# A fused two-layer transformer block on one core: the row maxima of the attention made 22 tiles ahead, from products of 32 rows on pairs of TensorE's row groups

## What is computed

```python
x = x + attention(layernorm(x))      # 16 heads of 8, rotary positions, softmax over 1024 keys
x = x + fp4_ffn(layernorm(x))        # blockwise quantised linear layers, silu(gate) * up
x = x + state_space(layernorm(x))    # softplus, a scan over the sequence, 32 states
x = x + moe(layernorm(x))            # 8 experts, the two best of each token
# the attention, for each batch b and head h:
attn = softmax(einsum('bhqd,bhkd->bhqk', q, k) * scale)
out  = einsum('bhqk,bhkd->bhqd', attn, v)
```

## Time and profile before

| what | us |
|---|---|
| median of 3 runs (1035.95 to 1038.92) | 1038.09 |
| the profiled execution | 1043.72 |
| its span of instructions | 1041.9 |
| ahead of the first product for maxima | 0 to 51.6 |
| maxima of pass 0 | 51.6 to 89.4 |
| passes 0 to 7 | 89.4 to 474.3 |
| FFN, state space and experts | 474.3 to 1041.9 |

### The profile page before, as it was taken

The page is one execution under the profiler, slowest core; times in us unless marked ns, Lnnn a source line. Parts: engine busy times, 40 slices in busy tenths (PEclk is TensorE's granted clock), DMA queues, the critical chain, the costliest instruction groups (busy, mean ns, idle before and its releaser), DMA issues. The chain is left out here.

```text
span 1041.9 us, 12586 instructions
## 1 busy us (share of the span) xinstructions
PE 858.3 (82%) x3695; PEld 401.7 (39%) x3703; DVE 848.1 (81%) x779; ACT 589.2 (57%) x913; POOL 273.1 (26%) x147
## 2 busy tenths in 40 slices
PE   5589999989999949985575565877777479999998
PEld 2212222222222212222444422322223266888886
DVE  6699888878888838855868789999999873888886
ACT  2304777767777727784132453444444166888885
POOL 3700000000000000010100157899999710122110
PEclk9857999999999969998586578899999877999999
DMA  7450010110102030002100232455455002232111
GB/s 177 126 138 1 11 57 12 57 47 31 44 28 57 12 102 12 11 11 62 34 0 6 81 106 83 159 178 170 167 172 178 2 0 84 62 110 71 60 61 41
DMA packets 37976, 73.51 MB, mean 71 GB/s; under 512 B 7298, under 2 KB 21626, under 8 KB 36890
## 3 DMA queue, kind: packets, MB, share of 16 engines
q1 hardware_dynamic: 37922, 72.82, 22.7%
HBM read 62.50 MB, written 8.85 MB: 68 GB/s over the span
## 5 line engine op out<-in xcount | busy, mean ns | idle before, releaser
L1004 DVE TENSOR_REDUCE nmax<-ps 128x1 f32<-128x1024 f32 x256 | 301.2, 1219 | 59.5 <-PE ps L1333 59.5
L765 ACT ACTIVATE prob<-ps 128x512 f32<-128x512 f32 x512 | 265.7, 605 | 139.4 <-PE ps L1352 139.2
L1333 PE MATMUL ps<-ks,qs 96*128 96x512 bf16 x512 | 206.6, 417 | 30.5 <-DVE nmax L1004 18.1
L1352 PE MATMUL ps<-qs,ks 96*128 96x512 bf16 x512 | 195.3, 390 | 7.2 <-ACT prob L765 3.3
L683 POOL TENSOR_TENSOR hc<-hst,cbr 128x1024 f32<-128x1024 f32 x64 | 152.6, 2408 | 10.1 <-DVE hst L1127 7.4
L1127 DVE TENSOR_TENSOR_SCAN hst<-ps,dbx 128x1024 f32<-128x1024 f32 x64 | 144.8, 2279 | 0.2
L1531 PE MATMUL ps<-hc,ident 128*128 128x512 f32 x256 | 128.9, 628 | 8.4 <-POOL hc L683 7.4
L1369 PE MATMUL ps<-prob,vq 128*16 128x512 f32 x1024 | 134.1, 601 | 0.8 <-ACT prob L765 0.7
L868 ACT ACTIVATE ps<-dt,a_neg 128x1024 f32<-128x1024 f32 x64 | 71.5, 1117 | 99.7 <-DVE hst L1127 99.6
L1216 DVE TENSOR_TENSOR act_l<-act_t,act_h 128x1024 fp32r<-128x1024 f32 x64 | 91.0, 1431 | 36.6 <-ACT act_h L937 36.6
L1352 PEld LDWEIGHTS ps<-qs,ks 96*128 96x128 bf16 x512 | 49.7, 99 | 165.6 <-ACT prob L765 117.7
(11 more groups left out here) (178 smaller groups left out, 1043.6 us busy)
## 6 DMA issues: line engine op xcount, KB each, us to landing
cbr<-s_dram SPq DMA_DIRECT2D x64, 512.0 KB, 4.1
gate<-c_dram SPq DMA_DIRECT2D x8, 1024.0 KB, 7.4
qs<-q_dram SPq DMA_DIRECT2D x18, 288.0 KB
ks<-k_dram SPq DMA_DIRECT2D x54, 96.0 KB
o_dram<-o_sb SPq DMA_DIRECT2D x16, 256.0 KB, 2.0
wf<-in_L_ffn_w SPq DMA_DIRECT2D x8, 256.0 KB, 2.9
wfq<-in_L_ffn_w SPq DMA_DIRECT2D x8, 256.0 KB, 3.1
q_dram<-parts SPq DMA_DIRECT2D x16, 96.0 KB, 1.9
```

The source lines that it names most:

```text
L765: nc.scalar.activation(prob[:, n % 8], ps[:, 4 + (first + n) % 3], ACT.Exp, scale=ATT_SCALE).then_inc(s_exp, 1)
L1004: nc.vector.tensor_reduce(nmax[:, half, n:n + 1], ps[:, 2 * (t % 2):2 * (t % 2) + 2, :], AX.XY, ALU.max, negate=True).then_inc(s_max, 1)
L1333: mm = nc.tensor.matmul(ps[:, 2 * (t % 2) + kk], qs[p][:, half, h, q * P:(q + 1) * P], ks[p][:, kk, h, :], start=True, stop=True)
L1352: nc.tensor.matmul(ps[:, 4 + (first + n) % 3], ks[p][:, kt // 4, j, kt % 4 * P:(kt % 4 + 1) * P], qs[p][:, half, j, :], start=True, stop=T ...
```

## The change

1. The maxima run 22 tiles ahead (LEAD), not 32. Ahead of pass 0 stand 22 tiles; steps 0 to 4 of each pass make tiles 22 to 31 of the pass itself, and steps 5 to 15 make tiles 0 to 21 of the next pass. So pass 7 has ten tiles in its first five steps.
2. From pass 1 on, a tile is made differently (`score_pair`): two heads by 512 keys, each head one product with 32 rows (two bfloat16 parts of q against two of k, all four combinations), in two of the four groups of 32 rows of TensorE, into two banks. There are as many tiles as before, with two products each. VectorE reduces a tile to two columns (one for each head), and a new operation on 128x16 takes the minimum over the two key halves (the values are negated). Pass 0 keeps the old form.
3. The operands `qm` and `km` lie head by head in groups of 32 rows and are filled by `load_heads`: 24 DMAs for a pass (12 for each half), each of 16 or 32 rows of 1 KB.
4. SyncE's queue is put in a new order: in pass it first the maxima of its own second half, then the 24 small loads for pass it+2, the output half, the maxima of the next pass's first half, the second output half, then `load` for it+3. The second four of the stores of q and k parts go into pass 0. The last three passes load nothing.
5. The reload of batch 0's sums is split: `load_out(0)` stands in pass 4, `load_denominators(0)` in pass 5, and VectorE inverts the denominators between the maxima of passes 5 and 6.
6. TensorE and SyncE have all passes written out, without a loop. ScalarE keeps its loop of two rounds, VectorE loops over passes 1 to 5.
7. In pass 7 `project_out(0)` goes from step 1 to 6, `turn_weights` from 8 to 12, and `turn_first_x` behind the pass; ScalarE's counterparts move likewise.

```diff
+PASS_TILES = QUAD * KT
+LEAD = 22
+        HEAD_LOADS = 16 * 2 * 3 * QUAD
+            def load_heads(it, p, f):
+                for h in range(QUAD):
+                    q, k = (t[bass.ds(it, 1), f].rearrange("o n (d h) t -> (o n d) h t", h=QUAD)[0:2 * HD, h]
+                            for t in (q_dram, k_dram))
+                    sp.dma_start(km[p][32 * h:32 * h + 32, f], k.unsqueeze(0).to_broadcast([2, 2 * HD, BANK])).then_inc(s_qm[p], 16)
+                    for a in range(2):
+                        sp.dma_start(qm[p][32 * h + 16 * a:32 * h + 16 * a + 16, f],
+                                     q[HD * a:HD * a + HD].unsqueeze(0).to_broadcast([2, HD, BANK])).then_inc(s_qm[p], 16)
...
-            for p in range(SETS):
-                load(p, p)
-            for u in range(CHUNKS, 2 * CHUNKS):
-                store_parts(u)
-            for n in range(CHUNKS):
-                sp.wait_ge(s_parts_out[n], 16 * QUAD * 2)
+            load(0, 0)
+            load(1, 1)
+            load_heads(1, 1, 0)
             store_maxima(0, 0, 0)
-            store_maxima(0, 0, 1)
-            def one_pass(it, p, more, again=None):
+            load_heads(1, 1, 1)
+            load(2, 2)
+            def one_pass(it, p, more, again=None, meanwhile=None):
+                store_maxima(it, p, 1)
+                if it + 2 < PASSES:
+                    for f in range(2):
+                        load_heads(it + 2, (p + 2) % SETS, f)
+                if it == 0:
+                    for u in range(CHUNKS, 2 * CHUNKS):
+                        store_parts(u)
+                    for n in range(CHUNKS):
+                        sp.wait_ge(s_parts_out[n], 16 * QUAD * 2)
+                store_out(it, 0)
                 if more:
                     store_maxima(it + 1, (p + 1) % SETS, 0)
-                store_out(it, 0)
+                if meanwhile:
+                    meanwhile()
+                store_out(it, 1)
                 if again is not None:
                     sp.wait_ge(s_pv, STEPS * (it + 1))
                     load(again, p)
-                store_out(it, 1)
-                if more:
-                    store_maxima(it + 1, (p + 1) % SETS, 1)
...
+            for it in range(PASSES):
+                one_pass(it, it % SETS, it < PASSES - 1, it + SETS if it + SETS < PASSES else None,
+                         {4: lambda: load_out(0), 5: lambda: load_denominators(0)}.get(it))
...
                         if whole:
                             nc.vector.tensor_reduce(nmax[:, half, n:n + 1], ps[:, 2 * pair:2 * pair + 2, :],
                                                     AX.XY, ALU.max, negate=True).then_inc(s_max, 1)
+                        else:
+                            nc.vector.tensor_reduce(nmax_k[:, half, kk, 2 * pair:2 * pair + 2, qt], ps[:, 2 * pair:2 * pair + 2, :],
+                                                    AX.X, ALU.max, negate=True).then_inc(s_max, 1)
...
+                        nc.vector.tensor_tensor(nmax[:, half], nmax_k[:, half, 0].rearrange("p h q -> p (h q)"),
+                                                nmax_k[:, half, 1].rearrange("p h q -> p (h q)"), ALU.min).then_inc(s_mstep, 1)
...
             inverse_denominators(0)
+            maxima(PASSES - 2)
             maxima(PASSES - 1)
...
+            def score_pair(it, p, u):
+                half, qt, kk, pair = u // 16, u % 16 // 4, u % 4 // 2, u % 2
+                pe.wait_ge(s_max, 32 * it + u - 1)
+                for n in range(2):
+                    rows = slice(32 * (2 * pair + n), 32 * (2 * pair + n + 1))
+                    mm = nc.tensor.matmul(ps[:, 2 * pair + n], qm[p][rows, half, qt * P:(qt + 1) * P],
+                                          km[p][rows, kk, :], start=True, stop=True)
+                mm.then_inc(s_score, 1)
...
-                        for t, kk in todo[len(todo) * j // 4:len(todo) * (j + 1) // 4]:
-                            score_half(it + 1, (p + 1) % SETS, t, kk)
+                        for tile in todo[len(todo) * j // 4:len(todo) * (j + 1) // 4]:
+                            if tile[0] == 0:
+                                score_half(*tile, 0)
+                                score_half(*tile, 1)
+                            else:
+                                score_pair(*tile)
...
-            for t in range(32):
+            for t in range(LEAD):
                 score_half(0, 0, t, 0)
                 score_half(0, 0, t, 1)
-            with pe.Fori(0, PASSES // SETS) as r:
-                for p in range(SETS):
-                    one_pass(SETS * r + p, p, 4 * STEPS * p, True, r + 1 + (p + 1) // SETS)
-            one_pass(PASSES - 2, 0, 0, True, PASSES // SETS + 1)
+            for it in range(PASSES - 1):
+                one_pass(it, it % SETS, 4 * STEPS * it, True, it // SETS + 1)
...
-            one_pass(PASSES - 1, 1, 4 * STEPS, False, between={1: lambda: project_out(0), 8: turn_weights, 12: turn_first_x})
+            one_pass(PASSES - 1, 1, 4 * STEPS, False, PASSES // SETS + 1, between={6: lambda: project_out(0), 12: turn_weights})
+            turn_first_x()
```

More of the change, by code:

```diff
@@ L127, in build_kernel @@
         qs, ks = ([pair[n] for pair in stacks] for n in range(2))
+        qm, km = ([sb(f"{w}{n}", [P, 2, BANK], BF16) for n in range(SETS)] for w in ("qm", "km"))
         prob = sb("prob", [P, 8, BANK])
@@ L136, in build_kernel @@
         nmax = sb("nmax", [P, 2, 16])
+        nmax_k = sb("nmax_k", [P, 2, 2, QUAD, 4])
         nmax_p = sb("nmax_p", [P, 32], BF16)
@@ L140, in build_kernel @@
         den = sb("den", [P, BATCH, HEADS * SEQ // P])
[L141 removed]
+        rden = sq[:].rearrange("p (b t) c -> p b (t c)", b=BATCH)
         num = sb("num", [P, TOKENS])
@@ L229, in build_kernel @@
         s_qk = [sem(f"s_qk{n}") for n in range(SETS)]
+        s_qm = [sem(f"s_qm{n}") for n in range(SETS)]
         s_score = sem("s_score")
@@ L564, in load_out, with load_denominators @@
                 sp.dma_start(num[:, b * SEQ:(b + 1) * SEQ], rows[:, 0:HD]).then_inc(s_num, 16)
+            def load_denominators(b):
                 sp.wait_ge(s_rden, b + 1)
@@ L570, in load_out @@
                 sp.sem_inc(s_ready, 1)
-            with sp.Fori(0, PASSES // SETS) as r:
-                for p in range(SETS):
-                    one_pass(SETS * r + p, p, True, (SETS * r + p + SETS) % PASSES)
-            load_out(0)
-            one_pass(PASSES - 2, 0, True)
-            one_pass(PASSES - 1, 1, False)
+            for it in range(PASSES):
+                one_pass(it, it % SETS, it < PASSES - 1, it + SETS if it + SETS < PASSES else None,
+                         {4: lambda: load_out(0), 5: lambda: load_denominators(0)}.get(it))
             load_out(1)
+            load_denominators(1)
             def load_expert(e, p):
@@ L816, in _ @@
             one_pass(PASSES - 1, 4 * STEPS, {
-                4: lambda: norm_act(1, 0),
-                9: turned_weights,
-                13: lambda: (turned_x(0, 0), turned_x(1, 1))})
+                8: lambda: norm_act(1, 0),
+                13: turned_weights})
+            turned_x(0, 0)
+            turned_x(1, 1)
             for p in range(4):
@@ L1015, in _ @@
             maxima(0)
-            with dve.Fori(1, PASSES - 1) as it:
+            with dve.Fori(1, PASSES - 2) as it:
                 maxima(it)
@@ L1336, in score_half, with tiles_ahead @@
                     mm.then_inc(s_score, 1)
+            def score_pair(it, p, u):
[6 more added lines that the diff above has]
+                mm.then_inc(s_score, 1)
+            def tiles_ahead(it, p, s, more):
+                for n in range(MAX_TILES):
+                    t = LEAD + MAX_TILES * s + n
+                    if t < PASS_TILES:
+                        yield it, p, t
+                    elif more:
+                        yield it + 1, (p + 1) % SETS, t - PASS_TILES
             def one_pass(it, p, first, more, loads=None, between={}):
@@ L1344, in one_pass @@
                         pe.wait_ge(s_nrow[half], 64 * (it + 1))
-                    if more and s == 0:
-                        pe.wait_ge(s_qk[(p + 1) % SETS], LOADS * loads)
-                    todo = [(MAX_TILES * s + n // 2, n % 2) for n in range(2 * MAX_TILES)] if more else []
+                    if more and LEAD + MAX_TILES * s == PASS_TILES:
+                        pe.wait_ge(s_qm[(p + 1) % SETS], HEAD_LOADS * loads)
+                    if s == 0:
+                        pe.wait_ge(s_qk[p], LOADS * loads)
+                    todo = list(tiles_ahead(it, p, s, more))
                     for j in range(QUAD):
@@ L1353, in one_pass @@
                                          qs[p][:, half, j, :], start=True, stop=True).then_inc(s_st, 1)
-                        for t, kk in todo[len(todo) * j // 4:len(todo) * (j + 1) // 4]:
-                            score_half(it + 1, (p + 1) % SETS, t, kk)
-                        if s >= 1 and j == (QUAD - 1 if more else QUAD - 2):
```

(7 more changed lines are left out.)

22 lines of the change are left out of this document (13 added, 9 removed).

## The result

The changed kernel takes 1010.39 us in the median of four runs (1005.62 to 1012.23), the kernel before 1038.51 beside it (1035.95 to 1040.88): a ratio of 0.972, interval 0.968 to 0.976. The forecast was 1005.7, within 978 to 1021. The profiled execution took 1012.23, its span 1010.4.

What follows compares the result with a forecast made beforehand. TensorE's own stream was taken to set the 2.815 us step, VectorE having 16% of slack. Terms -11.8, -12.3, -14.6, -1.0, +4.0 and +3.3 sum to -32.4, from 1038.1 to 1005.7 us, range 978 to 1021.

Steps and rivals of the forecast that it cites:

- ahead of pass 0, from the first reduction: Ahead of pass 0: ten tiles fewer at VectorE's pace of 1.18 us a tile, -11.8 us.
- the step, where the form is new: Steps 5 to 15 of pass 0 and passes 1 to 6: 107 steps from 2.815 to 2.70 us, -12.3 us.
- the stall in pass 6, less the reciprocal: Pass 6: the earlier denominators' load removes 15.6 us of stall, 1.0 left for reciprocal and tail, -14.6 us.
- the loops: Passes 2 and 3: TensorE's and SyncE's branches go, ScalarE's stays; -1.0 us, ends 0 and -5.3.
- SyncE's queue in pass 0: End of pass 0: small loads and 16 stores of parts delay the next maxima, +4 us, ends 0 and 9.
- pass 7 and behind it: Pass 7 and behind: ten tiles, wait for weights, x copies, less the moved x transposes; +3.3 us, ends 0 and +7.
- rival 2: Steps with pairs: products of a pair run in turn, step 3.12 us, kernel 1047 us, slower than before; chance 0.10.
- the third bank's wait: In the step: falls on the moment when it is due, about 0.6 us after the first exponential starts.
- rival 3: SyncE is the bound: 1.0 us per small load, late maxima, clock falling at each boundary, about 1043 us; chance 0.07.
- step 12: Pass 7: quantised weights come late as VectorE's chain starts 13.3 us later; wait 1.2 us, sign 1 to 3.
- VectorE didn't take over: Denies the rival that VectorE sets the pace if row tiles change without the drain: pass 39.8 us, kernel 982; chance 0.16.

Runs made afterwards that it cites:

- the undone lead: Maxima 32 tiles ahead again instead of 22, against the changed kernel with its stores of parts moved ahead of pass 0: 1014.73 us.
- the kernel with both pairs together: Changed kernel with both pairs of a step behind the second score product, four changes of form per step instead of five: 1009.92 us, ratio 0.974 to the kernel before.
- the fastest kernel: ScalarE looping over one pass seven times, banks begun anew each pass, against the changed kernel with stores of parts ahead of pass 0: 999.29 us.

## Why the prediction was right

Its steps against the two profiled executions, in us, each pass counted from its first exponential to the next pass's:

| term | forecast | measured |
|---|---|---|
| ahead of pass 0, from the first reduction | -11.8 | -11.7 (37.4 to 25.7) |
| the step, where the form is new | -12.3 | -10.5 |
| the stall in pass 6, less the reciprocal | -14.6 | -15.0 |
| the loops | -1.0 | -1.7 |
| SyncE's queue in pass 0 | +4.0 | +8.7, in a second execution +3.9 |
| pass 7 and behind it | +3.3 | +3.9 |
| the rest up to the FFN | | +1.0 |
| the FFN and behind it | 0 | -6.2 |
| sum | -32.4 | -31.5 in the profiled pair, -28.1 in the medians |

*Ahead of pass 0.* Right to 0.1, and shown by the undone lead.

*The step.* 2.70 forecast and 2.70 measured, out of three guesses that each held: products of a pair side by side, 0.1 for each change of form, VectorE hidden. The two experiments with one row group show the first (3.12 as forecast for rival 2), the old form gives its worth. The term is still 1.8 too large: 107 steps were counted as if each gained 0.115. Pass 6 has 2.76 and gains 1.0 where an undisturbed pass gains 1.65; and the latter isn't 16 x 0.115 = 1.84, since the steps at the ends of halves gain another amount: the two at the middle of a pass take 5.69 together in both kernels. The prediction saw the third bank's wait falling on the moment when it is due; in pass 6 it falls 0.06 late.

*The stall.* Right in size; the reciprocal cost 0.5 in pass 5 (44.42 against 43.90), where 1.0 was left for it. The early reload alone brought 12.1 in the medians.

*The loops.* Passes 2 and 3 had 5.3 above an undisturbed pass and have 3.7 (2.2 and 1.5). As forecast, ScalarE's branch took TensorE's place, and the wait moved from the earlier trace rows into a wait for exponentials. No run puts TensorE's loop back, so this term rests on the two traces.

*SyncE's queue.* The place was right and the size was not. A small load's issue takes 0.575, less than the 0.65 taken; but one issue among the stores of parts was held for an extra 1.5 us or so, so TensorE began pass 1 3.2 late. To that the prediction put no clock: it said that a low clock inside passes isn't forecast, and kept "the clock falls at each boundary" for rival 3. A wait of 2 to 3 us ahead of a pass brought it in 11 of the 12 cases in these traces (not behind the 2.49 of the kernel with both pairs together), and it cost 5.5 in this execution, 1.4 in the other. By the first execution the term is 8.7, close to the end of 9 given for it; by the second it is 3.9 (2.5 of wait and 1.4 of clock). That this meets the 4 forecast is luck: the forecast had 4 of wait and no clock.

*Pass 7.* It took 1.9 more, as put: 2.0 for the ten tiles (the kernel of lead 32), where 1.6 was put, and the rest -0.1, where 0.3 was put. Two steps waited: 0.5 at `project_out` for `num`, which stands behind VectorE's last tile and tail, and 0.8 at step 12 for the weights (1.2 put, 1 to 3 named as the sign); and the FFN begins 1.9 later behind the pass (x transposes and two copies ahead of the table load), where 1.4 was put. The reason given for step 12 was that VectorE's chain starts later on account of the ten tiles. The kernel of lead 32 has the same wait without them, from the place of `project_out(0)` alone, so the tiles aren't needed for it; in the changed kernel both stand in the way.

*What wasn't in the sum.* 5.9 us in the FFN stretch, whose code is the same. In the profiled kernels here it took 108.7 to 114.6, and the long ones have more of it under the low clock (65 us in the kernel before, 48 in the changed one). It doesn't go with the change alone: 114.1 with the old form, 112.9 in the fastest kernel, 108.7 and 108.9 in the two executions of the changed one. Why it falls where it does stays open. The forecast's 1005.7 was 4.7 below the measured median. In the profiled pair the errors cancel (-32.4 and -31.5), and that nearness is luck: up to the FFN the change brought 25.3, and the FFN stretch made up for it; the second execution got there 6 us earlier. The medians of the single experiments make up most of the whole: 9.1 for the lead, 8.7 for the form and 12.1 for the reload, less 4.8 for the stores in pass 0, are 25.1, and 26.8 with the loops' 1.7 from the traces, of 28.1. Their bases differ, so this is a check and no exact sum.

The rivals: VectorE didn't take over, since the two changes around a pair (0.19 to 0.22) cost nearly the slot that it saves (0.22); the pairs do run side by side; and SyncE is the bound nowhere but in pass 0. The chances had one slip: 0.86 for faster counts rival 3 in, though its own price of 1043 is slower.

## What to carry to other kernels

Count a change of form on TensorE as half a product: small products pay when several are set side by side behind one change, and then only until the engine that drains them becomes the bound, its tail at the end of a block included. Price a wait at the start of a dense stretch with the low clock that may follow it, and as a range, not at its own length. A queue in program order is checked where it carries a one-time job besides its regular one, and where a loop's end shows idle time, a shorter round is worth a trial.

## What the runs showed of the hardware

At the full clock, two products of 32 rows in different row groups took 0.39 us together (starts 3 to 4 ns apart), in the same group 0.60 (0.23 apart); one alone takes 0.38. Four of them, in four groups, took hardly longer to the next product than two (0.33 against 0.32).

Each change measured here between full products and row or column tiles cost 0.09 to 0.12 us on TensorE, in both directions.

With a stall of TensorE of 2.1 to 3.2 us came a low clock of very different length: 3.4 to 6.8 us with the old form (6.8 in the kernel before, from 229.8), 3.4, 6.8, 10.2 and 13.7 with pairs, once none (behind 2.49 us), and 177.5 in the one run with both products in one group. In that run TensorE was busy without a break, at half the clock. What decides it, no run here tells.

A loop's end after three passes cost ScalarE 2.1 us, TensorE 3.6; after a body of one pass ScalarE showed none.

Among the 16 stores of parts, one issue was held for 0.6 to 1.5 us in each of the five traces in which they stand in pass 0 behind the small loads, and none in the seven in which they stand ahead of pass 0. Why, no run tells.

ScalarE's written-out code started a step's first exponential 0.06 us later than the looped code (0.486 against 0.426 behind the score product).
